# A digit block moved behind two index searches in a kernel of DCT, attention and product-key experts

## The reference

```python
def reference(x, Wq, bq, ln_g, ln_b, keys0, keys1, expert_down, expert_up):
    h = tok(x)                                   # x: 32 clips of 40000 samples, zero-padded
    h = h + attn(layernorm(h))
    h = h + ffn(layernorm(h), Wq, bq, ln_g, ln_b, keys0, keys1, expert_down, expert_up)
    return h                                     # [32, 313, 128]

def tok(x):                                      # frames of 128, times a 128 x 128 DCT matrix
    return einsum('bfh,kh->bfk', frames, D)

def attn(x):                                     # per clip, 313 x 313 scores
    return softmax(x @ x.T, axis=2) @ x

def ffn(hidden_states, ...):                     # 8 heads, QD = 64, HALF = 32, 64 keys, K = 16
    q = layernorm((hidden_states @ Wq.T + bq).reshape(b, s, 8, 64)) * ln_g + ln_b
    s0 = l2norm(q[..., :32]) @ l2norm(keys0).T   # 64 scores
    s1 = l2norm(q[..., 32:]) @ l2norm(keys1).T   # 64 scores
    sc0, ix0 = top_k(s0, 16)
    sc1, ix1 = top_k(s1, 16)
    cs = (sc0[..., :, None] + sc1[..., None, :]).reshape(..., 256)
    ci = (ix0[..., :, None] + ix1[..., None, :]).reshape(..., 256)
    fs, pos = top_k(cs, 16)
    fi = take_along_axis(ci, pos)                # a sum of two key numbers: 0 to 126
    w = softmax(fs)
    inner = einsum('bsd,bshkd->bshk', hidden_states, expert_down[fi])
    return einsum('bshk,bshko->bso', gelu(inner) * w, expert_up[fi])
```

## Time and profile before

| | |
|---|---|
| median of 3 runs | 2086.8 us (2083.2 to 2092.77) |
| the profiled execution | 2086.99 us, its span 2085.2 us |
| DVE busy | 1925.5 us (92%) |
| PE busy (matmuls) | 1701.8 us (82%) |
| POOL busy | 1554.2 us (75%) |
| ACT busy | 1217.5 us (58%) |
| mean granted TensorE clock | 0.77 of full |

### The profile page before, as it was taken

How to read it: one execution, slowest core, us unless ns; L and a number is a source line. 1 busy time by engine, 2 the same in 40 slices (tenths; PEclk the granted TensorE clock), 3 DMA queues, 4 the chain that set the end, 5 groups by cost and what they waited for, 6 DMA issues and landing times.

```text
span 2085.2 us, 48099 instructions
## 1 busy us (share of the span) xinstructions
PE 1701.8 (82%) x11423; PEld 1296.2 (62%) x11423; DVE 1925.5 (92%) x15878; ACT 1217.5 (58%) x3851; POOL 1554.2 (75%) x2561
## 2 busy tenths in 40 slices
PE   5567888888889898898888898888988989788766
PEld 3335576756767576675667667565765757566556
DVE  3299999999999999999999999999999999999992
ACT  3345656666565566655566665666665556665454
POOL 2238787886878788787878868788787767878765
PEclk9676878768787777877788678876878777787666
DMA  1000000000000000000000000000000000000000
GB/s 35 13 9 2 19 7 8 20 6 19 6 19 7 6 19 9 19 6 18 8 6 19 9 17 9 13 12 6 19 7 19 9 9 16 7 13 9 6 6 11
DMA packets 46672, 24.86 MB, mean 12 GB/s; under 512 B 4955, under 2 KB 46116, under 8 KB 46390
## 3 DMA queue, kind: packets, MB, share of 16 engines
q1 hardware_dynamic: 46390, 21.80, 3.7%
HBM read 11.52 MB, written 10.26 MB: 10 GB/s over the span
## 4 chain that ended last, share of the span: by engine, by line
PE 38%; DVE 30%; ACT 16%; POOL 9%; issue 5%; SPq 0%; another core or an unknown queue 0%; DMA 0%; POOLq 0%; DVEq 0%; ACTq 0%
PE QB L531 8%; DVE alpha L1046 5%; PE FB L449 5%; PE FB L440 4%; PE SC L480 4%; ACT WD L732 4%; DVE idx L1030 4%; DVE idx L1033 4%; DVE hrest L1024 3%; PE QB L519 3%; ACT hi L672 3%; PE FB L421 3%; DVE vals L1028 2%; DVE vals L1021 2%; POOL sa L762 2%
## 5 line engine op out<-in xcount | busy, mean ns | idle before, releaser
L892 POOL TENSOR_TENSOR bw<-beta,wp 128x1024 bf16<-128x1024 bf16 x240 | 508.1, 2148 | 117.2 <-ACT wp L718 117.2
L531 PE MATMUL QB<-bw,alpha 128*128 128x48 bf16 x5120 | 555.0, 278 | 32.2 <-issue 32.2
L531 PEld LDWEIGHTS QB<-bw,alpha 128*128 128x128 bf16 x5120 | 523.1, 151 | 73.9 <-issue 65.5
L732 ACT ACTIVATE WD<-QB 32x96 f32<-32x96 f32 x1280 | 307.7, 240 | 76.4 <-PE QB L531 65.1
L1046 DVE TENSOR_SCALAR alpha<-hi 128x1024 bf16<-128x1024 bf16 x640 | 276.0, 501 | 0.0
L480 PE MATMUL SC<-WK,hidT 128*128 128x512 f32 x320 | 223.2, 787 | 50.6 <-ACT stdT L664 43.7
L1030 DVE FIND_INDEX8 idx<-vals,sraw 128x8 uint32<-128x64 f32 x1280 | 250.9, 219 | 0.0
L1033 DVE FIND_INDEX8 idx<-vals,hrest 128x8 uint32<-128x64 f32 x1280 | 250.7, 220 | 0.0
L1024 DVE MATCH_REPLACE8 hrest<-vals,sraw 128x64 f32<-128x64 f32 x1280 | 249.6, 208 | 0.0
L840 POOL TENSOR_TENSOR ci<-idxf 128x64 f32<-128x64 f32 (+3 forms) x400 | 124.3, 347 | 135.8 <-DVE beta L1052 135.6
L725 ACT ACTIVATE ofin<-QB 128x128 f32<-128x128 f32 x80 | 22.2, 278 | 281.0 <-PE QB L531 278.3
(11 more groups left out here) (205 smaller groups left out, 3963.5 us busy)
## 6 DMA issues: line engine op xcount, KB each, us to landing
res<-h_scratch SPq DMA_DIRECT2D x80, 64.0 KB, 1.8
xin<-in_x SPq DMA_DIRECT2D x32, 128.0 KB
h_scratch<-h2n SPq DMA_DIRECT2D x32, 128.0 KB
out<-ofin SPq DMA_DIRECT2D x64, 64.0 KB, 1.5
h_scratch<-h2n SPq DMA_DIRECT2D x32, 28.5 KB
out<-ofin SPq DMA_DIRECT2D x16, 57.0 KB
xin<-in_x SPq DMA_DIRECT2D x32, 28.0 KB
xin<-in_x SPq DMA_DIRECT2D x32, 0.2 KB
```

What stands on the lines that cost most here:

```text
L531: last = mm(bank[:, 48 * u:48 * u + 48], alpha[:, buf, a, :, 8 * p + u], bwv[:, :, a, :, 8 * p + u], start=(a == 0), stop=(a == 1))
L732: last = A(WD[r, RING[(t - 4) % NT], :, 8 * p:8 * p + 8], blocks[r, :, :, g], ACT.Copy)
L892: last = tt(bw[:, buf, NY * i:NY * i + NY, :], beta[:, buf, :, :], wp[:, buf, i, :].unsqueeze(1).to_broadcast([128, NY, 256]), ALU.mult)
```

## The change

DVE's digit block becomes a function of its own, `digits`, and is called in phase 2, behind both index searches and ahead of the candidates of phase 3; `norms` moves with it. The sums `zs` and `rz` stay in phase 1. ACT's `hi` moves from the head of phase 0 to its end, behind `zexp`, m, `wexp`, the first weight part and `idxf` (in phase 0 the copies of the first WD group come behind it). POOL's `ci` no longer waits for `beta`. No instruction is added or removed but waits.

```diff
@@ ACT slot @@
             def slot(k, t, p):
                 n = NT * k + t
-                if p == 0 and exists(k, t, 3):
-                    act.wait_ge(s["eb_full"], n - 2)
-                    after(act, s["alpha_full"], n - 3)
-                    for c in range(NS):
-                        last = A(hi[:, c, :], STE, ACT.Identity, bias=cdig[:, c:c + 1])
-                    last.then_inc(s["his_full"], 1)
                 if p == 0 and exists(k, t, 2):
                     buf = RING[(t - 2) % NT]
                     act.wait_ge(s["c2_full"], n - 1)
...
                     act.wait_ge(s["halves_full"], n)
                     after(act, s["ci_full"], n - 1)
                     A(idxf[:], idx[:, buf, :, :], ACT.Identity, bias=cquart[:]).then_inc(s["idxf_full"], 1)
+                if p == 0 and exists(k, t, 3):
+                    act.wait_ge(s["eb_full"], n - 2)
+                    after(act, s["alpha_full"], n - 3)
+                    for c in range(NS):
+                        last = A(hi[:, c, :], STE, ACT.Identity, bias=cdig[:, c:c + 1])
+                    last.then_inc(s["his_full"], 1)
@@ POOL slot @@
                 if p == 1 and exists(k, t, 1):
                     buf = RING[(t - 1) % NT]
-                    if exists(k, t, 3):
-                        pool.wait_ge(s["beta_full"], n - 2)
                     pool.wait_ge(s["idxf_full"], n)
                     cells(ci[:, buf, :, :], idxf[:], s["ci_full"])
@@ DVE @@
+            def digits(k, t):
+                n = NT * k + t
+                if exists(k, t, 3):
+                    old = RING[(t - 3) % NT]
+                    dve.wait_ge(s["his_full"], n - 2)
+                    after(dve, s["beta_full"], n - 3)
+                    V.scalar_tensor_tensor(out=lo[:], in0=STE, scalar=BASE, in1=hi[:, 0, :], op0=ALU.add, op1=ALU.subtract
+                                           ).then_inc(s["lo_full"], 1)
+                    after(dve, s["quads_full"], 4 * (n - 4))
+                    h8 = hi[:].rearrange("p c (m q) -> p c m q", q=NQ)
+                    a8 = alpha[:, old, :, :, :].rearrange("p a (g c x) q -> p c (a g) x q", g=NG, c=NS)
+                    for xx in range(NX // NS):
+                        last = V.tensor_scalar(a8[:, :, :, xx, :], h8, BASE + float(NY * xx), None, ALU.is_equal)
+                    last.then_inc(s["alpha_full"], 1)
+                    after(dve, s["bw_full"], n - 4)
+                    dve.wait_ge(s["lo_full"], n - 2)
+                    for y in range(NY):
+                        last = V.tensor_scalar(beta[:, old, y, :], lo[:], y - 1.5, None, ALU.is_equal)
+                    last.then_inc(s["beta_full"], 1)
...
-                if p == 1:
-                    digits, sums = exists(k, t, 3), exists(k, t, 2)
-                    old = RING[(t - 3) % NT]
-                    if digits:
-                        dve.wait_ge(s["his_full"], n - 2)
...
-                        last.then_inc(s["beta_full"], 1)
+                if p == 2:
+                    digits(k, t)
                     if t == NT - 1 and exists(k, t, -1):
                         norms(k + 1)
+                if p == 1:
+                    sums = exists(k, t, 2)
                     if sums:
                         dve.wait_ge(s["cand_chain"], 31)
```

## The result

The changed kernel takes 2111.3 us (median of 4, 2109.59 to 2114.13), the kernel before 2086.31 us on the same chip: ratio 1.0117, 95% interval 1.009 to 1.0144. It is 1.2% slower. The forecast was 2091 us, with 2048 to 2122 as its range. The profiled execution has a span of 2112.3 us, 27.1 more than before.

What follows compares the result with a forecast made beforehand. DVE, busy for 1925.5 of 2085.2 us, was taken as the bound. 2087 plus 8 for the moved digits less 2.3 in the drain gave 2093, said as 2091 (no change); range 2048 to 2122.

Steps and rivals of the forecast that it cites:

- the side to which I gave 0.33: Whole kernel: the chance given to a time slower by over 0.5%.
- the absorber: DVE's two waits for PE's variance, 2.2 us in two pairs, said to shrink when DVE comes later.
- waits for `hi`, old stretch of `alphas` and `betas`: DVE's `lo` waits and `alphas` and `betas` stretched beside POOL go: 12.8 us won in two pairs.
- slot 4, `alphas` beside Yw and Ye: Slot 4: `alphas` wait out POOL's `wz`, Yw and Ye, 3.3 us a slot, 6.6 in two pairs.
- slot 0: Slot 0: `alphas` meet Yw and Ye, and `zs` may wait for `zexp`; 3.1 us a slot, 6.2 for two.
- slot 2: Slot 2: the row seed waits for ACT's squares, 3.5 us, plus 1 for Ye's tail; 4.5 in two pairs.
- part 1: DVE's digit block behind the index searches: 17.3 us paid, 12.8 won, 1 left after absorption; +8 in the run.
- Parts 2 and 3: ACT's `hi` later, no gain to PE's and ACT's round; POOL's `ci` freed, bw behind late `beta`; counted at nothing.
- The drain: At the kernel's end: the sums come first, so POOL's `wz` no longer waits 2.34 us for `rz`; -2.3.
- (a): Faster rival: PE's and ACT's round sets the pace and DVE follows; 35 us won, 2052; chance 0.30.
- (b): Slower rival: the `alphas` hold off POOL's Ye in slot 0, so PE starts 1.9 later; 2115; chance 0.15.
- (c): Slower rival: part 1's DVE account with nothing absorbed, 4.5 us in two pairs, +36; 2121; chance 0.15.

Runs made afterwards that it cites:

- `norms` in the middle: The changed kernel with `norms` between slot 4's two index searches (first pair: behind the digits); 2124.89 us, ratio 1.0159 to the kernel before.
- `norms` early: The changed kernel with `norms` kept in phase 1 ahead of the sums; 2169.32 us, ratio 1.0377 to the kernel before.
- the kernel with slots 1, 2 and 3: The kernel before with the new order (all three parts) in slots 1, 2 and 3 alone, `norms` as before; 2129.85 us, ratio 1.019.

## Why the prediction held, and where it failed

The time lay inside the range, on the side to which I gave 0.33. The point, 2091, was 20 us low. That the range held is partly luck: two terms that I had at nothing cost 8.3 us in two pairs, and three that I had too large gave 7.4 back. Two steps of the sum had no row behind them, the 1 us that I took as what the absorber leaves of 4.5 (2.2 of waits leave 2.3), and the last rounding, from 2093 to 2091. The terms of the DVE account for two pairs, forecast and measured:

| term | forecast | measured |
|---|---|---|
| waits for `hi`, old stretch of `alphas` and `betas` | -12.8 | -12.8 (3.1 + 7.7 + 2.0) |
| slot 4, `alphas` beside Yw and Ye | +6.6 | +5.9 |
| slot 0 | +6.2 | +3.2 (`alphas` 1.25, `zs` 1.9) |
| slot 2 | +4.5 | +0.8 (`alphas`; the seed didn't wait) |
| variance waits, an absorber | up to -2.2 | -1.1 |
| `norms` beside bw | 0 | +7.0 |
| the variances' seed, `xh` of 40 columns | 0 | +1.3 |
| sum | +1 | +4.3 (the stretch grew by 3.7; the 0.6 between is not traced) |

The mechanism of slot 4 came out as worked: `wz` 13.4 us into it (forecast 13.5), the last `alpha` done at 19.9 (20.2). One reading was off without weight in the sum: the `alphas` before took 2.76 us in three of the ten slots, not in one, and 3.03 to 4.40 in the others.

**The step that failed** is in part 1: "`norms` moves with the block; its consumer is POOL's work in the next slot, hidden." I asked who waits for its result and not what it stands beside. The rule for that was in my own text, one paragraph up: a DVE instruction waits until the running POOL instruction ends. In the new order bw starts when the last `beta` is done, 0.13 to 0.24 us behind it in 19 of 20 slots, so what DVE does right behind the `betas` meets it. (At the old place `norms` stood behind the `betas` too, but POOL's bw came only after `wz`, Yw and Ye.) That term is 7.0 us in two pairs, 59 us of DVE's time in the run. With `norms` alone moved, some 72 us of such time made the kernel 47 us longer.

**The terms that were too large** covered for it. Slot 0: one of two slots waited for `zexp`, and the `alphas` mostly missed Ye. Slot 2: the squares ended 4.7 and 4.5 us into the slots after (1122.21 and 1245.36; the slots start at 1117.5 and 1240.9), not 7 to 10. I read this as DVE's long slot 4 letting ACT and PE run ahead (argued; the kernel with `norms` in the middle fits it). Where slot 4 is short (`norms` in the middle) the waits of 5.3 us for `hid` and 2.9 for `zexp` are there, of the kind that the prediction worked out (4.2 and 0.6 us). So these terms were right as a mechanism for a kernel in which slot 4 is not the longest.

**Parts 2 and 3.** That `hi` has room and that POOL's `ci` comes free held. "I count both at nothing" for bw behind the late `beta` did not: in slot 3 and slot 2 I named it, slot 0 I didn't name, and there PE stood mostly 2.8 to 4.3 us ahead of slot 1's quads. In the changed kernel DVE hides it (98.5% busy in the ten slots); that it is a part of what slows the versions without the `norms` term is argued from their QB waits, not shown.

**The drain.** POOL's wait of 2.34 us for `rz` is gone, but the time isn't: from the start of the last slot with index searches (2001.3 before, 2026.6 after) to the end it is 83.9 us before and 85.7 after. POOL's bw waits for the late `beta` there: it stood idle for 6.39 us ahead of the one at 2044.19, and the last `beta` ended at 2044.06.

**The rivals.** (a) did not come: relieved DVE meets the other round at once. (b) did not hit Ye in slot 0 of the changed kernel (2.15 us), but its mechanism showed with `norms` early. (c), at 2121, was 10 us off where the forecast was 20 off, for a partly wrong reason: DVE was what all wait for, with another term in the account. The test that I had set for (c), a variance that never waits, was not met: its wait halved (1.1 us in ten slots, 2.2 before).

**What stays open.** With `norms` short the waits that come up are named above (`zexp`, the squares, `hi`, bw), but no run removes what makes ACT and PE late, so the second limit isn't priced. Why the kernel with slots 1, 2 and 3 is granted a lower clock, when PE's work is the same, wasn't settled. No version that I ran beats the kernel before.

## What to carry to other kernels

When a block moves, list every instruction that moves with it and ask of each what will run beside it at the new place; a consumer that has time says nothing of an instruction's own length. On DVE a costly place for short work is right behind the signal that starts POOL's long instructions. And behind a nearly full engine a second round can lie so close that relieving the first gives nothing: run the kernel with the suspected cost gone before counting it as a gain.

## What the runs showed of the hardware

- A DVE instruction of 0.2 us (128 x 80) lasts about as long as the POOL instruction that it meets: 2.01 and 2.18 us beside bw of 2.22 and 2.14, with one tensor input or with two (1.80 and 2.07).
- It goes the other way too, and for more than one instruction: a POOL instruction of 0.20 us took 3.34 beside eight `alphas` and four `betas` (3.3 us in all). Beside long POOL instructions (Yw 1.17, Ye 2.35) the two engines took turns, and eight `alphas` lasted 5.73 us in place of 2.76.
- In that case POOL's long instructions hardly show the contention: bw had a mean of 2.24 us with the `alphas` beside it, where the `alphas` went to 1076 ns, and 2.13 without.
